# Moving elementwise work between VectorE, ScalarE and GpSimd in an attention and feed-forward kernel on 8 cores

## The chip, the cores and the metric

The kernel runs on 8 cores of one Trainium2 chip. Each core computes 1024 of the 8192 rows of the input by itself; the cores exchange nothing. The time is the device time of the slowest core in microseconds (us). Below, TensorE is PE, VectorE is DVE, ScalarE is ACT, GpSimd is POOL and SyncE is SP, as in the profile's rows.

## What is computed

```python
x = L0_attn_query_input                                   # (2, 4096, 2048) float32
x = x + attn(layernorm(x))
x = x + ffn(layernorm(x))

def attn(query_input):                                    # 16 heads of 128, 1024 stored patterns
    q = (rms_norm(query_input, nqw) @ W_in.T).reshape(B, S, H, D) @ W_q.T
    k = stored_patterns @ W_k.T
    v = stored_patterns @ W_v.T
    probs = softmax(einsum(q * sigmoid(beta), k))
    return rms_norm(einsum(probs, v), norm_retrieved_w) + query_input

def ffn(x):                                               # int8 weights with scales, 8192 wide
    return (silu(x @ w_gate * s_gate) * (x @ w_up * s_up)) @ w_down * s_down
```

## The kernel before

The program has seven stages, one after another, and between two of them stands `barrier()` (lines 201 to 217): PE, ACT and DVE each issue one tiny instruction and wait until all three have. Every engine's instructions are written out by hand in queue order (`Rt` puts one on PE's queue, `Rs` on ACT's, `Rv` on DVE's, `Rg` on POOL's, `Ry` on SP's), and every dependence is a semaphore that counts up: `cT` for PE, `cS` for ACT, `cV` for DVE, `cG` for POOL, and `vv` and `ss` for chains inside DVE and ACT. Nothing is reordered at run time: an engine that waits holds up all that stands behind it on its queue.

1. Layer norm of x, its transpose, and the product of W_in and W_q.
2. The q projection (lines 451 to 495). 16 blocks `hc`, each 32 matmuls of 128x512 into a ring of four PSUM tiles of 1024 floats; each tile is then read out by one ACT instruction (line 491) that multiplies by `bvec` (the sigmoid of beta) and writes bf16. PE waits for the readout of block hc-4 before it writes the same tile.
3. k and v of all heads.
4. Attention, head by head.
5. What is called the G stage here (lines 668 to 919): the divided softmax, the second RMS norm, the sums with x, the layer norm of the feed-forward part and its transpose, for 8 tiles `j` of 128 rows.
6. Gate and up projections, 64 blocks (lines 921 to 989).
7. Down projection in 4 quarters of 512 columns, with the last sum and the stores of the output (lines 991 to 1110).

The G stage is a software pipeline. Iteration k works on tiles k, k-1 and k-2 and puts this on the queues:

- DVE: `G_V2(k-1)` (lines 766 and 768, two instructions of one column: the mean square and its reciprocal), `G_BN(k-2)` (four bn_stats, lines 838 and 834, one bn_aggr, two instructions of one column, the last on line 845), `G_P1(k)` (lines 727 and 721: 12 of the 16 heads of the tile, 128 columns each, times the reciprocal of the softmax sum), `G_T3(k-1)` (line 788, one scalar_tensor_tensor of 2048 columns), the left half of the sum `G_AD(k-1)` (line 802, 1024 columns), `G_SE(k-2)` (line 898, the readout of the transposed tile).
- ACT: `G_sqrt(k-1)` (775), `G_SQ(k-2)` (lines 854, 858, 862 with one column and 870, the normalised tile), `G_xar(k)` (709), `G_P1s(k)` (lines 747 and 741: the other 4 heads), `G_S1(k)` (758: the sum of squares).
- POOL: the right half of the sum `G_AD(k-1)` (line 813, 1024 columns).
- PE: `G_T1(k-2)` (lines 888 and 884, 16 transposes). SP: loads of x and stores of the sum to `x1sp`.

The waits that tie them together: `G_V2(k-1)` waits for `G_S1(k-1)` on ACT; `G_BN(k-2)` waits for both halves of the sum of tile k-2; `G_SQ(k-2)` on ACT waits for `G_BN(k-2)`, and `G_xar(k)`, `G_P1s(k)` and `G_S1(k)` stand behind it on ACT's queue; `G_T3(k-1)` stands behind `G_P1(k)` on DVE's queue; the sum of tile k-1 waits for `G_T3(k-1)`.

Of the kernel before, what the change touches and what calls it, by code (L numbers as in the profile page):

```python
# [12 lines left out]
AF = mybir.ActivationFunctionType  # L13
ALU = mybir.AluOpType
# [7 lines left out]
H = 16  # L22
# [23 lines left out]
def _build_nc():  # L46
# [26 lines left out]
    with ctx:  # L73
# [12 lines left out]
        bvec = ctx.enter_context(nc.sbuf_tensor("bvec_s", [128, 1], F32))  # L86
# [88 lines left out]
        dX = [sems["dX0"], sems["dX1"]]  # L175
        dSo = [sems["dSo0"], sems["dSo1"]]
        sXr = [sems["sXr%d" % i] for i in range(4)]
        cT = sems["cT"]
        cS = sems["cS"]
        cV = sems["cV"]  # L180
        cG = sems["cG"]
# [8 lines left out]
        def Rs(f): ops["s"].append(f)  # L190

        def Rv(f): ops["v"].append(f)
# [5 lines left out]
        def wait(R, sem, val):  # L198
            R(lambda En, h=sem.h, v=val: En.wait_ge(h, v))
# [50 lines left out]
        t = cS.tick()  # L250
# [4 lines left out]
        t = cT.tick()  # L255
# [3 lines left out]
        t = cV.tick()  # L259
# [196 lines left out]
        qT = bfv(O_QT, 16384)  # L456
        q_evac_val = [None] * H
        nqw_val = [None] * EC
        for ec in range(EC):
            t = cS.tick()  # L460
# [3 lines left out]
        for hc in range(H):  # L464
            pq = PS[:, (hc % 4) * 1024:(hc % 4) * 1024 + 1024]
            if hc == 1:
                wait(Rt, cS, nqw_val[EC - 1])
            if hc >= 4:
                wait(Rt, cS, q_evac_val[hc - 4])
            for half in range(2):  # L470
                for ec in range(EC):
                    if hc == 0 and half == 0:
                        wait(Rt, cS, nqw_val[ec])
                    lastmm = half == 1 and ec == EC - 1
                    if lastmm:
                        t1 = cT.tick()
                        Rt(lambda En, pq=pq, ec=ec, half=half, hc=hc:
                           En.matmul(pq[:, half * 512:half * 512 + 512],
                                     W2T3[:, ec, hc * 128:(hc + 1) * 128],
                                     nqT3[:, ec, half * 512:half * 512 + 512],  # L480
                                     start=(ec == 0), stop=(ec == EC - 1)).then_inc(cT.h, 1))
                    else:
                        Rt(lambda En, pq=pq, ec=ec, half=half, hc=hc:
                           En.matmul(pq[:, half * 512:half * 512 + 512],  # L484
                                     W2T3[:, ec, hc * 128:(hc + 1) * 128],
                                     nqT3[:, ec, half * 512:half * 512 + 512],
                                     start=(ec == 0), stop=(ec == EC - 1)))
            wait(Rs, cT, t1)
            t2 = cS.tick()
            Rs(lambda En, hc=hc, pq=pq:  # L490
               En.activation(qT[:, hc * 1024:(hc + 1) * 1024], pq, AF.Identity,
                             scale=bvec[:]).then_inc(cS.h, 1))
            q_evac_val[hc] = t2
        barrier()

# [204 lines left out]
        def G_xar(j):  # L700
            xre = f32v(O_XRE[j % 2], 2048)
            xar = f32v(O_XA[j % 2], 2048)
            wait(Rs, sA[j % 2], g_ld[j])
            if j >= 2:
                wait(Rs, cG, adv_g[j - 2])
                wait(Rs, cV, adv_v[j - 2])
            t = cS.tick()
            Rs(lambda En, xar=xar, xre=xre, j=j:
               En.activation(xar, xre, AF.Identity, scale=a1s[:, j:j + 1],
                             bias=bbs[:, j:j + 1]).then_inc(cS.h, 1))  # L710
            xaval[j] = t

        def G_P1(j):
            t0 = f32v(O_T0[j % 2], 2048)
            if j >= 2:
                wait(Rv, cS, sq1val[j - 2])
            for hh in range(4, H):
                if hh == H - 1:
                    t = cV.tick()
                    Rv(lambda En, j=j, hh=hh, t0=t0:  # L720
                       En.tensor_scalar(t0[:, hh * 128:(hh + 1) * 128],
                                        A3[:, j, hh * 128:(hh + 1) * 128],
                                        rscol[:, hh * NT + j:hh * NT + j + 1], None,
                                        ALU.mult).then_inc(cV.h, 1))
                else:
                    Rv(lambda En, j=j, hh=hh, t0=t0:
                       En.tensor_scalar(t0[:, hh * 128:(hh + 1) * 128],
                                        A3[:, j, hh * 128:(hh + 1) * 128],
                                        rscol[:, hh * NT + j:hh * NT + j + 1], None,
                                        ALU.mult))  # L730
            p1val[j] = t

        def G_P1s(j):
            t0 = f32v(O_T0[j % 2], 2048)
            if j >= 2:
                wait(Rs, cV, t3val[j - 2])
            for hh in range(4):
                if hh == 3:
                    t = ss.tick()
                    Rs(lambda En, j=j, hh=hh, t0=t0:  # L740
                       En.activation(t0[:, hh * 128:(hh + 1) * 128],
                                     A3[:, j, hh * 128:(hh + 1) * 128], AF.Identity,
                                     scale=rscol[:, hh * NT + j:hh * NT + j + 1]).then_inc(ss.h, 1))
                    p1sval[j] = t
                else:
                    Rs(lambda En, j=j, hh=hh, t0=t0:
                       En.activation(t0[:, hh * 128:(hh + 1) * 128],
                                     A3[:, j, hh * 128:(hh + 1) * 128], AF.Identity,
                                     scale=rscol[:, hh * NT + j:hh * NT + j + 1]))
# [42 lines left out]
        def G_AD(j):  # L792
            t3r = f32v(O_T3[j % 2], 2048)
            xar = f32v(O_XA[j % 2], 2048)
            x1t = f32v(O_X1[j % 2], 2048)
            if j >= 2:
                wait(Rv, cS, x1nval[j - 2])
                wait(Rv, dX[j % 2], dxval[j - 2])
            wait(Rv, cV, t3val[j])
            t = cV.tick()  # L800
            Rv(lambda En, x1t=x1t, t3r=t3r, xar=xar:
               En.tensor_add(x1t[:, 0:1024], t3r[:, 0:1024],
                             xar[:, 0:1024]).then_inc(cV.h, 1))
            adv_v[j] = t
            wait(Rg, cV, t3val[j])
            wait(Rg, cS, xaval[j])
            if j >= 2:
                wait(Rg, cV, bnval[j - 2])
                wait(Rg, cS, x1nval[j - 2])
                wait(Rg, dX[j % 2], dxval[j - 2])  # L810
            t = cG.tick()
            Rg(lambda En, x1t=x1t, t3r=t3r, xar=xar:
               En.tensor_add(x1t[:, 1024:2048], t3r[:, 1024:2048],  # L813
                             xar[:, 1024:2048]).then_inc(cG.h, 1))
            adv_g[j] = t

        def G_SP(j):
            x1t = f32v(O_X1[j % 2], 2048)
            wait(Ry, cV, adv_v[j])
            wait(Ry, cG, adv_g[j])  # L820
            dma(Ry, dX[j % 2], x1sp_d[j], x1t)
            dxval[j] = dX[j % 2].n

        def G_BN(j):
            x1t = f32v(O_X1[j % 2], 2048)
            W = 32 + j * 16
            ST = 176 + (j % 2) * 24
            wait(Rv, cG, adv_g[j])
            wait(Rv, cV, adv_v[j])
            for i in range(4):  # L830
                if i == 3:
                    t = vv.tick()
                    Rv(lambda En, i=i, x1t=x1t, ST=ST:
                       En.bn_stats(wrk[:, ST + i * 6:ST + (i + 1) * 6],
                                   x1t[:, i * 512:(i + 1) * 512]).then_inc(vv.h, 1))
                else:
                    Rv(lambda En, i=i, x1t=x1t, ST=ST:
                       En.bn_stats(wrk[:, ST + i * 6:ST + (i + 1) * 6],
                                   x1t[:, i * 512:(i + 1) * 512]))
            wait(Rv, vv, t)  # L840
            bnval[j] = VC(
                lambda En, W=W, ST=ST: En.bn_aggr(wrk[:, W + 6:W + 8], wrk[:, ST:ST + 24]),
                lambda En, W=W: En.tensor_scalar(wrk[:, W + 8:W + 9], wrk[:, W + 7:W + 8],
                                                 EPS_LN, None, ALU.add),
                lambda En, W=W: En.reciprocal(wrk[:, W + 9:W + 10], wrk[:, W + 8:W + 9]),
                final=cV)

        def G_SQ(j):
# [15 lines left out]
            wait(Rs, ss, t)  # L864
            if j >= 2:
                wait(Rs, cT, tr2_val[j - 2])
            wait(Rs, cV, adv_v[j])
            t = cS.tick()
            Rs(lambda En, x1n=x1n, x1t=x1t, W=W:
               En.activation(x1n, x1t, AF.Identity, scale=wrk[:, W + 10:W + 11],  # L870
# [311 lines left out]
```

## Time and profile before

| | us |
|---|---|
| time of the kernel, median of 2 runs (2129.28 to 2130.96) | 2130.12 |
| time of the profiled execution | 2131.07 |
| span of its slowest core (core 5), first to last instruction | 2129.5 |
| spans of the eight cores | 2110.6 to 2129.5 |
| PE busy | 1804.7 (85%) |
| ACT busy | 633.1 (30%) |
| DVE busy | 211.1 (10%) |
| POOL busy | 176.3 (8%) |

A span runs from the first to the last instruction of one core; the time of the profiled execution is 1.6 us more than the span of its slowest core. A busy share over the whole span is a mean over seven stages with different limits: how an engine that is busy 8% of the span can still matter is read from the stage in which it works.

### The profile page before, as it was taken

Reading aid. Unit: us, or ns where it says so; the run is one execution under the profiler, and the core shown is the slowest. Engines: PE = TensorE matmul, PEld = TensorE weight load, DVE = VectorE, ACT = ScalarE, POOL = GpSimd, SP = SyncE. Lnnn points to the kernel's source line nnn. Section 1 sums busy time; section 2 is a strip of 40 time slices with the busy share of each in tenths; the row PEclk is TensorE's granted clock in tenths of the full one; section 3 lists DMA queues with packets and bytes.
Section 4 is the critical chain, followed back from the end, with each engine's and each line's share of the span. In section 5 each row is a group of like instructions: output and inputs, shape, how many; then the busy total and the mean of one; then the engine's idle time right before and its main releaser. Section 6 shows DMA issues by size and latency. Waiting matters only on the chain.

```text
span 2129.5 us, 20649 instructions; the slowest of 8 cores (2110.6 to 2129.5 us)
## 1 busy us (share of the span) xinstructions
PE 1804.7 (85%) x8489; PEld 840.0 (39%) x8489; DVE 211.1 (10%) x448; ACT 633.1 (30%) x605; POOL 176.3 (8%) x239
## 2 busy tenths in 40 slices
PE   3489778888801799999999999999997979899795
PEld 2434333443401344444444444444443434344342
DVE  3300000000068100000000000000000020100202
ACT  4741365566556111111111111111114212222120
POOL 3200110000012100000000000000000010100101
PEclk8679768888855799999999999999998989999898
DMA  9600310000053212222221222222213131221301
GB/s 284 195 1 1 98 61 0 1 1 1 1 197 119 92 66 79 80 80 79 79 72 67 79 79 80 79 79 69 70 60 104 40 104 40 79 65 40 104 20 60
DMA packets 42370, 154.67 MB, mean 73 GB/s; under 512 B 6181, under 2 KB 6182, under 8 KB 36902
## 3 DMA queue, kind: packets, MB, share of 16 engines
q0 software_dynamic: 23984, 84.00, 11.6%
q1 hardware_dynamic: 18294, 69.35, 10.2%
q8 instruction: 69, 1.13, 0.2%
q14 instruction: 23, 0.19, 0.0%
HBM read 103.10 MB, written 16.78 MB: 56 GB/s over the span
## 4 chain that ended last, share of the span: by engine, by line
PE 79%; ACT 8%; DMA 6%; DVE 4%; issue 3%; POOL 1%; SPq 0%; DVEq 0%; ACTq 0%; POOLq 0%
PE PS L955 21%; PE PS L970 20%; PE PS L1095 19%; PE PS L484 5%; PE PS L578 3%; PE PS L593 3%; DMA out<-arena 2%; DMA arena<-patT 2%; ACT arena L622 2%; PE PS L642 1%; PE PS L615 1%; PE PS L609 1%; ACT arena L332 1%; ACT arena L404 1%; ACT arena L461 1%
## 5 line engine op out<-in xcount | busy, mean ns | idle before, releaser
L1095 PE MATMUL PS<-arena 128*128 128x512 bf16 x1956 | 451.3, 386 | 48.8 <-DVE arena L1034 39.8
L955 PE MATMUL PS<-arena 128*128 128x512 bf16 x2048 | 455.2, 381 | 5.3 <-DMA arena<-wu 5.3
L970 PE MATMUL PS<-arena 128*128 128x512 bf16 x1984 | 438.7, 379 | 0.0
L1095 PEld LDWEIGHTS PS<-arena 128*128 128x128 bf16 x1956 | 193.3, 99 | 291.6 <-issue 68.4
L955 PEld LDWEIGHTS PS<-arena 128*128 128x128 bf16 x2048 | 201.0, 98 | 248.9 <-issue 9.0
L979 ACT ACTIVATE arena<-PS,sgc_s 128x1024 bf16<-128x1024 f32 x64 | 71.3, 1114 | 735.5 <-PE PS L964 735.5
L970 PEld LDWEIGHTS PS<-arena 128*128 128x128 bf16 x1984 | 194.1, 98 | 234.1
L1062 ACT ACTIVATE arena<-arena 128x2048 bf16<-128x2048 int8 x64 | 121.6, 1908 | 345.0 <-PE PS L1084 336.6
L622 ACT ACTIVATE arena<-PS 128x1024 bf16<-128x1024 f32 x128 | 129.3, 1024 | 63.1 <-PE PS L609 63.1
L987 DVE TENSOR_TENSOR arena<-arena 128x1024 bf16<-128x1024 bf16 x64 | 44.3, 693 | 851.3 <-ACT arena L982 851.3
L484 PE MATMUL PS<-arena 128*128 128x512 bf16 x496 | 117.0, 390 | 8.2 <-ACT arena L461 8.2
L578 PE MATMUL PS<-arena,onemat_s 128*128 128x512 bf16 x256 | 85.8, 420 | 18.5 <-ACT arena L622 18.5
L232 POOL DMA_DIRECT2D arena<-wg x64 | 33.9, 529 | 807.2 <-PE PS L964 795.6
L888 PE MATMUL PS<-ident_s,arena 128*128 128x128 bf16 x120 | 14.1, 309 | 102.0 <-ACT arena L870 102.0
L593 PE MATMUL PS<-arena 128*128 128x512 bf16 x240 | 82.3, 423 | 0.0
L484 PEld LDWEIGHTS PS<-arena 128*128 128x128 bf16 x496 | 49.0, 99 | 73.4 <-issue 17.9
L982 ACT ACTIVATE arena<-PS,suc_s 128x1024 bf16<-128x1024 f32 x64 | 70.9, 1107 | 0.0
L1029 DVE TENSOR_TENSOR arena<-PS,arena 128x512 f32<-128x512 f32 x32 | 22.1, 691 | 473.1 <-PE PS L1084 436.6
L615 PE MATMUL PS<-arena 128*128 128x512 bf16 x128 | 58.0, 453 | 0.1
L609 PE MATMUL PS<-arena 128*128 128x512 bf16 x128 | 57.9, 452 | 0.0
L232 POOL DMA_DIRECT2D out<-arena x32 | 17.4, 543 | 486.0 <-DVE arena L1034 484.3
L813 POOL TENSOR_TENSOR arena<-arena 128x1024 f32<-128x1024 f32 x8 | 25.6, 3194 | 384.3 <-DVE arena L788 384.3
(110 smaller groups left out, 937.3 us busy)
## 6 DMA issues: line engine op xcount, KB each, us to landing
arena<-wg POOLq DMA_DIRECT2D x64, 512.0 KB, 3.5
arena<-wu POOLq DMA_DIRECT2D x64, 512.0 KB, 4.2
arena<-win SPq DMA_DIRECT2D x16, 1024.0 KB, 7.4
arena<-x SPq DMA_DIRECT2D x16, 1024.0 KB, 8.5
arena<-wd SPq DMA_DIRECT2D x64, 256.0 KB, 2.7
arena<-patT SPq DMA_DIRECT2D x16, 512.0 KB, 4.4
x1sp<-arena SPq DMA_DIRECT2D x8, 1024.0 KB, 4.2
arena<-x1sp POOLq DMA_DIRECT2D x32, 256.0 KB, 5.0
```

Of the source, the lines that this page charges most:

```text
L484: En.matmul(pq[:, half * 512:half * 512 + 512], W2T3[:, ec, hc * 128:(hc + 1) * 128], nqT3[:, ec, half * 512:half * 512 + 512], start=(ec ...
L578: En.matmul(PSS[:, half * 512:half * 512 + 512], onemat[:], eT[:, m * 1024 + half * 512:m * 1024 + half * 512 + 512], start=(m == 0), stop ...
L593: En.matmul(PU[:, half * 512:half * 512 + 512], vsb[:, (h * MC + m) * 128:(h * MC + m + 1) * 128], eT[:, m * 1024 + half * 512:m * 1024 + ...
L609: En.matmul(psb[:, half * 512:half * 512 + 512], kT[:, h * 1024 + mc * 128:h * 1024 + (mc + 1) * 128], qT[:, h * 1024 + half * 512:h * 102 ...
L615: En.matmul(psb[:, half * 512:half * 512 + 512], kT[:, h * 1024 + mc * 128:h * 1024 + (mc + 1) * 128], qT[:, h * 1024 + half * 512:h * 102 ...
L622: En.activation(eT[:, mc * 1024:(mc + 1) * 1024], psb, AF.Exp).then_inc(cS.h, 1))
L955: En.matmul(PG[:, half * 512:half * 512 + 512], wgb[:, hc * 128:(hc + 1) * 128], x1nT3[:, hc, half * 512:half * 512 + 512], start=(hc == 0 ...
L970: En.matmul(PU2[:, half * 512:half * 512 + 512], wub[:, hc * 128:(hc + 1) * 128], x1nT3[:, hc, half * 512:half * 512 + 512], start=(hc == ...
L979: En.activation(sgb, PG, AF.Silu, scale=sgc[:, ic:ic + 1]))
L982: En.activation(sub, PU2, AF.Identity, scale=suc[:, ic:ic + 1]).then_inc(cS.h, 1))
L1062: En.activation(wdb, wd8, AF.Copy).then_inc(cS.h, 1))
L1095: En.matmul(PS[:, j * 512:(j + 1) * 512], fuse3[:, ic, j * 128:(j + 1) * 128], wdb[:, c * 512:(c + 1) * 512], start=(ic == 0), stop=(ic == ...
```

## The change

It edits stages 2 and 5.

In stage 2 the 16 readouts of the q tiles go from ACT to DVE: line 491 becomes a `tensor_scalar` of 1024 columns from PSUM, and PE waits for `cV` in place of `cS`.

In the G stage `G_P1` keeps 9 heads on DVE instead of 12, and `G_P1s` does 7 on ACT instead of 4. DVE's half of the sum (line 802) is gone, and POOL adds all 2048 columns in one instruction (line 803 of the changed kernel). The waits for DVE's half are dropped or turned to POOL's counter: `adv_v[j]` now holds the value of `cG`.

```diff
             if hc >= 4:
-                wait(Rt, cS, q_evac_val[hc - 4])
+                wait(Rt, cV, q_evac_val[hc - 4])
...
-            wait(Rs, cT, t1)
-            t2 = cS.tick()
-            Rs(lambda En, hc=hc, pq=pq:
-               En.activation(qT[:, hc * 1024:(hc + 1) * 1024], pq, AF.Identity,
-                             scale=bvec[:]).then_inc(cS.h, 1))
+            wait(Rv, cT, t1)
+            t2 = cV.tick()
+            Rv(lambda En, hc=hc, pq=pq:
+               En.tensor_scalar(qT[:, hc * 1024:(hc + 1) * 1024], pq, bvec[:], None,
+                                ALU.mult).then_inc(cV.h, 1))
...
                 wait(Rs, cG, adv_g[j - 2])
-                wait(Rs, cV, adv_v[j - 2])
...
-            for hh in range(4, H):
+            for hh in range(7, H):
...
-            for hh in range(4):
-                if hh == 3:
+            for hh in range(7):
+                if hh == 6:
...
-            if j >= 2:
-                wait(Rv, cS, x1nval[j - 2])
-                wait(Rv, dX[j % 2], dxval[j - 2])
-            wait(Rv, cV, t3val[j])
-            t = cV.tick()
-            Rv(lambda En, x1t=x1t, t3r=t3r, xar=xar:
-               En.tensor_add(x1t[:, 0:1024], t3r[:, 0:1024],
-                             xar[:, 0:1024]).then_inc(cV.h, 1))
-            adv_v[j] = t
...
-               En.tensor_add(x1t[:, 1024:2048], t3r[:, 1024:2048],
-                             xar[:, 1024:2048]).then_inc(cG.h, 1))
+               En.tensor_add(x1t, t3r, xar).then_inc(cG.h, 1))
             adv_g[j] = t
+            adv_v[j] = t
...
-            wait(Ry, cV, adv_v[j])
             wait(Ry, cG, adv_g[j])
...
             wait(Rv, cG, adv_g[j])
-            wait(Rv, cV, adv_v[j])
...
-            wait(Rs, cV, adv_v[j])
+            wait(Rs, cG, adv_g[j])
```

DVE's queue in one steady iteration of the G stage, before, from `G_P1` to the next `G_BN` (each row is an instruction, what it writes and reads, and the semaphores it waits for):

```order
L727 TENSOR_SCALAR arena<-arena,rscol_s 128x128 [waits cS]
L727 TENSOR_SCALAR arena<-arena,rscol_s 128x128 x10
L721 TENSOR_SCALAR arena<-arena,rscol_s 128x128
L788 SCALAR_TENSOR_TENSOR arena<-arena,wrk_s 128x2048 [waits ss,dC,cG]
L802 TENSOR_TENSOR arena<-arena 128x1024 [waits cS,dX0,cV]
L898 COPY arena<-PS 128x16x128 [waits cT]
L766 TENSOR_SCALAR wrk_s<-wrk_s 128x1 [waits cS]
```

The same place in the changed kernel, where the line numbers have shifted (727 is 726, 721 is 720, 788 is 787, 898 is 886, 766 is 765, 768 is 767, 838 is 826):

```order
L726 TENSOR_SCALAR arena<-arena,rscol_s 128x128 [waits cS]
L726 TENSOR_SCALAR arena<-arena,rscol_s 128x128 x7
L720 TENSOR_SCALAR arena<-arena,rscol_s 128x128
L787 SCALAR_TENSOR_TENSOR arena<-arena,wrk_s 128x2048 [waits ss,dC]
L886 COPY arena<-PS 128x16x128 [waits cT]
L765 TENSOR_SCALAR wrk_s<-wrk_s 128x1 [waits cS]
L767 RECIPROCAL wrk_s<-wrk_s 128x1 [waits vv]
L826 BN_STATS wrk_s<-arena 128x6 [waits cG]
```

Three of the 128-column products and the sum of 1024 columns have left the queue, and bn_stats waits for POOL's counter alone.

ACT's queue in one steady iteration, before, from the normalised tile of `G_SQ` to the square root:

```order
L870 ACTIVATE arena<-arena,wrk_s 128x2048 [waits ss,cT,cV]
L709 ACTIVATE arena<-arena,bbs_s,a1s_s 128x2048 [waits sA0,cG,cV]
L747 ACTIVATE arena<-arena,rscol_s 128x128 [waits cV]
L747 ACTIVATE arena<-arena,rscol_s 128x128 x2
L741 ACTIVATE arena<-arena,rscol_s 128x128
L758 ACTIVATE arena,wrk_s<-arena 128x2048 [waits cV,ss]
L775 ACTIVATE wrk_s<-wrk_s 128x1 [waits cV]
```

And in the changed kernel (870 is 858, 709 is 708, 747 is 746, 741 is 740, 758 is 757, 775 is 774):

```order
L858 ACTIVATE arena<-arena,wrk_s 128x2048 [waits ss,cT,cG]
L708 ACTIVATE arena<-arena,bbs_s,a1s_s 128x2048 [waits sA0,cG]
L746 ACTIVATE arena<-arena,rscol_s 128x128 [waits cV]
L746 ACTIVATE arena<-arena,rscol_s 128x128 x5
L740 ACTIVATE arena<-arena,rscol_s 128x128
L757 ACTIVATE arena,wrk_s<-arena 128x2048 [waits cV,ss]
L774 ACTIVATE wrk_s<-wrk_s 128x1 [waits cV]
```

Three products more stand between the normalised tile and the sum of squares; the order is otherwise as it was.

## Rows read from the trace of the kernel before

**Rows 1.** The page: the chain that ended last, by engine.
```profile
PE 79%; ACT 8%; DMA 6%; DVE 4%; issue 3%; POOL 1%; SPq 0%; DVEq 0%; ACTq 0%; POOLq 0%
```

**Rows 2.** Windows, core 5: stretch, length, busy us (instructions) by engine, PEclk, DMA, GB/s.
```profile
587.25:705.50 118.25, 14.92 (x128) 13.02 (x128) 83.26 (x193) 66.71 (x98) 25.55 (x8) 0.50 0.41 151
...
635.55:647.97 12.42, 1.86 (x16) 1.63 (x16) 10.38 (x24) 8.15 (x12) 3.16 (x1) 0.50 0.45 165
```

**Rows 3.** Waits in the G stage: who waited for whom, us in total, times, longest.
```profile
ACT wrk_s L854 <- DVE wrk_s L845: 30.3, 8, 6.8
DVE wrk_s L766 <- ACT arena L758: 22.1, 8, 12.0
...
DVE wrk_s L838 <- POOL arena L813: 1.0, 1, 1.0
```

**Rows 4.** Timeline of DVE, one steady iteration: start, us, what [idle before <-releaser].
```profile
635.55 1.88 DVE L838 BATCH_NORM_STATS2 wrk_s<-arena 128x6 f32<-128x512 f32 x3
...
638.86 2.25 DVE L727 TENSOR_SCALAR arena<-arena,rscol_s 128x128 f32<-128x128 bf16 x11
641.02 0.28 DVE L721 TENSOR_SCALAR arena<-arena,rscol_s 128x128 f32<-128x128 bf16 x1
641.22 2.35 DVE L788 SCALAR_TENSOR_TENSOR arena<-arena,wrk_s 128x2048 f32<-128x2048 f32 x1
643.67 1.23 DVE L802 TENSOR_TENSOR arena<-arena 128x1024 f32<-128x1024 f32 x1
644.81 1.22 DVE L898 COPY arena<-PS 128x2048 bf16<-128x2048 bf16 x1
647.55 0.15 DVE L766 TENSOR_SCALAR wrk_s<-wrk_s 128x1 f32<-128x1 f32 x1 [1.52 <-ACT arena L758]
```

**Rows 5.** Timeline of ACT, the same iteration.
```profile
639.01 0.20 ACT L854 ACTIVATE wrk_s<-wrk_s 128x1 f32<-128x1 f32 x1 [3.17 <-DVE wrk_s L845]
...
640.10 2.09 ACT L870 ACTIVATE arena<-arena,wrk_s 128x2048 bf16<-128x2048 f32 x1 [0.20 <-ACT wrk_s L862]
...
644.08 0.97 ACT L747 ACTIVATE arena<-arena,rscol_s 128x128 f32<-128x128 bf16 x3
644.96 0.39 ACT L741 ACTIVATE arena<-arena,rscol_s 128x128 f32<-128x128 bf16 x1
645.44 1.91 ACT L758 ACTIVATE arena<-arena 128x2048 f32<-128x2048 f32 x1
```

**Rows 6.** Timeline of POOL: the first sum, one of a steady iteration, the last.
```profile
606.97 3.32 POOL L813 TENSOR_TENSOR arena<-arena 128x1024 f32<-128x1024 f32 x1 [322.18 <-DVE arena L788]
...
643.95 3.16 POOL L813 TENSOR_TENSOR arena<-arena 128x1024 f32<-128x1024 f32 x1 [9.21 <-DVE arena L788]
...
691.48 3.14 POOL L813 TENSOR_TENSOR arena<-arena 128x1024 f32<-128x1024 f32 x1 [7.05 <-DVE arena L788]
```

**Rows 7.** Timeline of DVE at the first and at the last tiles.
```profile
606.86 1.23 DVE L802 TENSOR_TENSOR arena<-arena 128x1024 f32<-128x1024 f32 x1
...
610.46 1.88 DVE L838 BATCH_NORM_STATS2 wrk_s<-arena 128x6 f32<-128x512 f32 x3 [0.95 <-POOL arena L813]
...
685.30 1.88 DVE L838 BATCH_NORM_STATS2 wrk_s<-arena 128x6 f32<-128x512 f32 x3
...
691.20 1.23 DVE L802 TENSOR_TENSOR arena<-arena 128x1024 f32<-128x1024 f32 x1
...
695.31 1.87 DVE L838 BATCH_NORM_STATS2 wrk_s<-arena 128x6 f32<-128x512 f32 x3
```

**Rows 8.** Groups by line and shape, POOL, core 5: busy us, mean ns | idle before.
```profile
L303 POOL CAST arena<-arena 128x2048 bf16<-128x2048 f32 x16 | 30.3, 1893 | 57.7 <-DMA arena<-win 37.1 <-PE PS L318 20.6
...
L517 POOL CAST arena<-arena 128x1024 bf16<-128x1024 f32 x16 | 16.6, 1040 | 176.8 <-DMA arena<-patT 176.8
```

**Rows 9.** Groups by line and shape: ACT and DVE of core 5, then DVE of core 0.
```profile
L491 ACT ACTIVATE arena<-PS,bvec_s 128x1024 bf16<-128x1024 f32 x16 | 17.8, 1114 | 92.7 <-PE PS L478 92.7
...
L1029 DVE TENSOR_TENSOR arena<-PS,arena 128x512 f32<-128x512 f32 x32 | 22.1, 691 | 473.1 <-PE PS L1084 436.6 <-DMA out<-arena 36.4
...
L1029 DVE TENSOR_TENSOR arena<-PS,arena 128x512 f32<-128x512 f32 x32 | 22.1, 690 | 480.6 <-PE PS L1084 432.6 <-DMA out<-arena 48.0
```

## The prediction

> **What bounds the kernel now.** I read the chain that ended last first: PE holds 79% of it, ACT 8%, DVE 4%, POOL 1% [rows 1]. The matmul stages are PE's, and the change takes nothing from PE. What it moves lies in two places, so I read these: the end of stage 2, and the G stage, from 587.25 to 705.5 us. There PE is busy 14.92 of 118.25 us, DVE 83.26, ACT 66.71, POOL 25.55 [rows 2]. No engine is near full: the stage is set by a loop of waits. The waits name it: ACT waits 8 times, 30.3 us in all, for DVE's line 845 (end of `G_BN`), DVE waits 8 times, 22.1 us, for ACT's line 758 (`G_S1`), and only once, 1.0 us, for POOL [rows 3].
>
> One steady iteration takes 12.42 us [rows 2]. I count from the start of bn_stats at 635.55 [rows 4]. ACT's line 854 starts 3.46 us later, at 639.01, the normalised tile at 640.10, the product of heads at 644.08, the sum of squares at 645.44 [rows 5]; DVE's line 766, released by it, at 647.55 [rows 4]; the next bn_stats starts 0.42 us behind it, at 647.97, the end of the window in [rows 2]. So the loop is `G_BN` on DVE, then `G_SQ`, `G_xar`, `G_P1s`, `G_S1` on ACT, then `G_V2` on DVE. The other DVE work of the iteration (`G_P1`, `G_T3`, its half of the sum, `G_SE`) stands beside it: DVE is through with it at 646.03 and idles 1.52 us [rows 4].
>
> **The change part by part.**
>
> *Three heads from DVE to ACT.* On ACT the products start 0.293 us apart (644.08 to 644.96 for three [rows 5]), so three more make 0.88 us, inside the loop. On DVE they start 0.196 us apart (638.86 to 641.02 for eleven [rows 4]); taking three away makes 0.59 us, but outside it. The loop through ACT goes from 12.42 to 13.30 us. Nothing covers the 0.88: ACT idles 3.17 us per iteration [rows 5], but ahead of line 854, and the products stand behind it on the same queue.
>
> *DVE's half of the sum.* Line 802 took 1.23 us [rows 4] beside the loop, followed by an idle DVE. Taking it away gives nothing directly.
>
> *The whole sum on POOL.* This adds a path: `G_BN` must wait for a POOL instruction twice as wide. How long is that? The trace shows only the half: 3.32, 3.16 and 3.14 us [rows 6]. But each ran beside line 802. The first, 606.97 to 610.29, began 0.11 us after line 802, which ended at 608.09; the others, at 643.95 and 691.48, began 0.28 us after it [rows 4, 6, 7]. From the end of line 802 to the end of POOL's half it is 2.20, 2.21 and 2.19 us. A longer overlap makes the instruction longer by exactly as much, so POOL did no work while line 802 ran. I read 2.20 us as the work on 1024 columns, and 4.40 us as that on 2048, since in the changed kernel no line 802 exists.
>
> The Trainium skill ("SBUF — State Buffer", section "Who interferes with whom") has a rule for this: a DVE instruction with two SBUF inputs and a GpSimd instruction that reads SBUF exclude each other for the whole instruction. By that rule the 2.20 us stand; the trace agrees. Its "GPSIMD Engine Reference" (section 3.1) gives 4.50 us for an fp32 add of 2048 columns; with that as an estimate the sum below would be 0.2 us more.
>
> Bounds: if part of the 2.20 is paid once, as in the casts (1.893 us for 2048 columns, 1.040 for 1024 [rows 8], so 0.19 us is fixed), the sum takes 4.21 us. If there is no exclusion and POOL is just slow, it is twice 3.15, 6.30 us. I take 4.40: it is twice what three rows agree on. Shorter than 4.21 is excluded, since it has twice the columns to do.
>
> Path through POOL, from bn_stats: `G_T3` starts after 5.67 us (641.22 minus 635.55), now 0.59 earlier, 5.08; POOL starts 2.73 us after that (643.95 minus 641.22); it runs 4.40; bn_stats follows 0.17 us after its end (610.29 to 610.46 [rows 6, 7]). Sum 12.38 us. That is 0.92 less than the 13.30 through ACT: in the steady iterations POOL is hidden, and it would decide from a duration of 5.32 us on.
>
> *Fill and drain,* where POOL is not hidden:
> - First bn_stats (610.46 before, released by POOL [rows 7]). ACT's products of tile 0 push all by 0.88, DVE's fewer products pull `G_T3(0)` by 0.59, so POOL starts at 606.97 + 0.29 = 607.26, ends at 611.66, and bn_stats starts at 611.83: +1.37 us.
> - Six iterations up to the seventh bn_stats at 685.30: 6 x 0.88 = +5.28 us.
> - Last bn_stats: 10.01 us after the seventh (695.31 [rows 7]). POOL starts as before at 691.48, 6.18 us after the seventh, then 4.40 and 0.17: 10.75. +0.74 us.
>
> Together +7.39 us. SP's load of tile k+2 stands ahead of the store that waits for POOL, and the store behind it is released by the same event as bn_stats, so SP delays nobody.
>
> *The q readout on DVE.* PE fills a tile in some 6.9 us and has a ring of four, so 15 of 16 readouts are covered; the last stands before a barrier. ACT takes 1.114 us [rows 9]. DVE with a PSUM input takes 0.691 us for 512 columns [rows 9], and line 802 1.23 for 1024 without PSUM [rows 7]: I take 1.23, +0.11 us. Bounds: 0.69 (if it runs at twice the rate) to 1.38 (twice 0.691): -0.42 to +0.27. No DVE work is queued there, so its wait holds up nobody.
>
> Sum: +7.5 us on the profiled 2131.07, 2138.6. That execution lies 0.95 us above the median of the runs, so the forecast is 2137.6.
>
> **The rivals.**
>
> A. *POOL is the new bound.* Without exclusion the sum takes 6.30 us; the iteration becomes 7.98 + 6.30 = 14.28, +1.86 six times, 11.2; the first bn_stats comes 1.37 + 1.90 = 3.3 later, the last 0.74 + 1.90 = 2.6 more. +17.1 us, with the readout 2147.3. For it: the half really took 3.15. Against it: the three rows that end 2.20 us after line 802. It decides above 5.32 us.
>
> B. *DVE is the bound of the G stage,* and not slower comes out: it is the busiest engine there with 83.26 us [rows 2], and 0.59 + 1.23 us leave it per tile. Eight tiles would give 14.6 us back: 2115.5. It decides if DVE, once released, has no idle time. Against it: the 1.52 us idle in each iteration and the 22.1 us of waits for ACT [rows 3, 4]. Removing work from an engine that waits gives nothing.
>
> C. *The waits for output stores in the last stage shift.* DVE waited 36.4 us there on core 5 and 48.0 us on core 0 of the same run [rows 9], and both ended within 0.5 us of each other. All cores reach this stage some 7 us later, so a shift in common should leave these waits alone; if they don't, up to 11.6 us go either way: 2126 to 2149. It cancels the loss only from 7.5 us on.
>
> **How the numbers follow.** Forecast (2135 to 2140.5, the bounds of POOL's 4.21 and the readout, and 2 us for run and store waits): 0.70. Rival A 0.15. Rival B 0.04. Rival C 0.10, half to each side. Something not named here 0.01. The range 2132 to 2148.5 takes in A and parts of C. The kernel's measurement tells about 2% from no change, 42.6 us: faster would be below 2087.5, slower above 2172.7, and no case reaches either. So faster 0.01, within 0.98, slower 0.01.
>
> **What would show it.** Right: in the G stage ACT's line 757 is followed by an iteration of 13.3 us; seven products 0.293 us apart; POOL's line 803 takes 4.4 us and DVE waits for it only at the first and last tile; the stage is 7 to 8 us longer; the last q readout takes 1.2 us. Wrong: bn_stats waits for POOL in every iteration (rival A), a period at or below 12.4 us (rival B), or a G stage that is 7 us longer with a total that isn't (rival C). The forecast falls if POOL's sum takes over 5.3 us, or if the ACT products of an iteration fit into its idle time.

## The result and the profile after

The changed kernel is slower by a third of a per cent, far less than the 2% from which the measurement tells a change. The median of its 11 runs is 2139.07 us, that of 10 runs of the kernel before, made beside them, 2133.54 us. Some executions of either kernel are 1.5 to 13% longer, with a lower granted clock; they are in these medians, and the ratio is taken without them: 1.0036, 95% interval 1.0025 to 1.0047, which is +7.7 us (5.3 to 10.0). The forecast was +7.5 us, 2137.6.

The profiled execution took 2132.41 us, less than any of the 11 runs and only 1.3 us more than the profile before, so its total says little. Measured from one barrier matmul of PE (line 208) to the next and averaged over the cores, the G stage grew from 117.6 to 125.2 us, the last stage shrank from 528.6 to 525.0, and every other stretch agrees within 0.4 us. In the nine profiles of the experiments the last stage took 526.2 to 529.1 us, so the small total is that stage's scatter. Of the G stage's 7.7 us, 1.0 lies in the wait for the first load of x, which scatters too (7.7 to 11.3 us from the barrier, by core). Behind this load the stage's length agrees within 0.1 us on all eight cores of an execution. I therefore read the change from there. The stage is measured from the start of ACT's first `xar` (line 709, in the changed kernel 708), which waits for the load of x, to PE's closing barrier matmul (line 208). Timeline of the kernel before, core 5:

```profile
596.27 2.09 ACT L709 ACTIVATE arena<-arena,bbs_s,a1s_s 128x2048 f32<-128x2048 f32 x1 [9.43 <-DMA arena<-x]
...
705.53 0.16 PE L208 MATMUL PS<-onesrow_s 1*1 1x1 bf16 x1 [1.48 <-DVE arena L898]
```

and of the changed kernel, core 2, the slowest of its profile:

```profile
595.58 2.09 ACT L708 ACTIVATE arena<-arena,bbs_s,a1s_s 128x2048 f32<-128x2048 f32 x1 [10.81 <-DMA arena<-x]
...
711.53 0.16 PE L208 MATMUL PS<-onesrow_s 1*1 1x1 bf16 x1 [1.48 <-DVE arena L886]
```

That is 109.26 us before and 115.95 after: +6.69 us. The chain of the whole program is PE's as before [rows 1]:

```profile
PE 78%; ACT 8%; DMA 5%; DVE 4%; issue 3%; POOL 1%; SPq 0%; DVEq 0%; ACTq 0%; POOLq 0%
```

Windows over the stage and over one iteration (columns as in [rows 2]: length, then busy us of PE, PE's weight loads, DVE, ACT, POOL):

```profile
585.00:711.60 126.60, 15.08 (x130) 13.09 (x129) 69.09 (x161) 73.71 (x122) 36.07 (x8) 0.50 0.37 141
624.43:637.60 13.17, 1.87 (x16) 1.63 (x16) 8.59 (x22) 9.03 (x15) 4.51 (x1) 0.50 0.41 151
```

DVE's work per iteration fell from 10.38 to 8.59 us and ACT's rose from 8.15 to 9.03 [rows 2], and the iteration grew from 12.42 to 13.17. The busiest engine was relieved and the stage got longer. The waits say why; against [rows 3]:

```profile
DVE wrk_s L765 <- ACT arena L757: 35.4, 8, 14.9
ACT wrk_s L842 <- DVE wrk_s L833: 30.1, 8, 7.6
...
DVE wrk_s L826 <- POOL arena L803: 1.4, 2, 0.7
```

DVE waits 13.3 us more for ACT than before, ACT as long as before for DVE, and for POOL DVE waits twice, 1.4 us in all, not in every iteration. One iteration on DVE, against [rows 4]:

```profile
624.43 1.88 DVE L826 BATCH_NORM_STATS2 wrk_s<-arena 128x6 f32<-128x512 f32 x3
...
627.74 1.66 DVE L726 TENSOR_SCALAR arena<-arena,rscol_s 128x128 f32<-128x128 bf16 x8
...
629.50 2.35 DVE L787 SCALAR_TENSOR_TENSOR arena<-arena,wrk_s 128x2048 f32<-128x2048 f32 x1
633.13 1.22 DVE L886 COPY arena<-PS 128x2048 bf16<-128x2048 bf16 x1 [1.28 <-PE PS L872]
637.24 0.15 DVE L765 TENSOR_SCALAR wrk_s<-wrk_s 128x1 f32<-128x1 f32 x1 [2.89 <-ACT arena L757]
```

and on ACT, against [rows 5]:

```profile
627.89 0.20 ACT L842 ACTIVATE wrk_s<-wrk_s 128x1 f32<-128x1 f32 x1 [3.10 <-DVE wrk_s L833]
...
632.91 1.84 ACT L746 ACTIVATE arena<-arena,rscol_s 128x128 f32<-128x128 bf16 x6
634.66 0.38 ACT L740 ACTIVATE arena<-arena,rscol_s 128x128 f32<-128x128 bf16 x1
635.13 1.91 ACT L757 ACTIVATE arena<-arena 128x2048 f32<-128x2048 f32 x1
```

ACT's wait of 3.1 us stands where it stood, ahead of line 842 (854 before), and all seven products lie behind it: from the first product to the sum of squares it is 2.22 us, before 1.36. POOL's sums, first, steady and last, against [rows 6]:

```profile
606.65 4.50 POOL L803 TENSOR_TENSOR arena<-arena 128x2048 f32<-128x2048 f32 x1 [322.70 <-DVE arena L787]
...
632.24 4.51 POOL L803 TENSOR_TENSOR arena<-arena 128x2048 f32<-128x2048 f32 x1 [8.84 <-DVE arena L787]
...
696.69 4.50 POOL L803 TENSOR_TENSOR arena<-arena 128x2048 f32<-128x2048 f32 x1 [7.09 <-DVE arena L787]
```

and bn_stats on DVE at the first, the seventh and the last tile, against [rows 7]:

```profile
611.25 1.88 DVE L826 BATCH_NORM_STATS2 wrk_s<-arena 128x6 f32<-128x512 f32 x3 [0.70 <-POOL arena L803]
...
690.51 1.88 DVE L826 BATCH_NORM_STATS2 wrk_s<-arena 128x6 f32<-128x512 f32 x3
...
701.29 1.88 DVE L826 BATCH_NORM_STATS2 wrk_s<-arena 128x6 f32<-128x512 f32 x3 [0.69 <-POOL arena L803]
```

Twice the columns took 4.50 us, not twice 3.15. The end of stage 2:

```profile
235.80 0.38 PE L478 MATMUL PS<-arena 128*128 128x512 bf16 x1
236.29 1.28 DVE L491 TENSOR_SCALAR arena<-PS,bvec_s 128x1024 bf16<-128x1024 f32 x1 [5.62 <-PE PS L478]
...
237.72 0.16 PE L208 MATMUL PS<-onesrow_s 1*1 1x1 bf16 x1 [1.54 <-DVE arena L491]
```

PE stood 1.54 us for the last readout; on the kernel before it was 1.47 us for ACT's.

### The profile page after: what moved, and what is told of

The parts are those of the page before. It is cut to its first block, busy times and chain, and to the rows that moved or that the text cites. A ratio compares the mean times of both kernels' runs of the same rounds, so it can differ in the third digit from the quotient of the medians.

```text
span 2130.9 us, 20446 instructions; the slowest of 8 cores (2121.1 to 2130.9 us)
## 1 busy us (share of the span) xinstructions
PE 1790.3 (84%) x8336; PEld 840.4 (39%) x8489; DVE 217.7 (10%) x432; ACT 622.6 (29%) x613; POOL 186.8 (9%) x239
## 3 DMA queue, kind: packets, MB, share of 16 engines
q8 instruction: 69, 1.13, 0.2%
## 4 chain that ended last, share of the span: by engine, by line
PE 78%; ACT 8%; DMA 5%; DVE 4%; issue 3%; POOL 1%; SPq 0%; DVEq 0%; ACTq 0%; POOLq 0%
PE PS L943 21%; PE PS L958 20%; PE PS L1083 19%; PE PS L484 5%; PE PS L578 3%; PE PS L593 2%; DMA out<-arena 2%; DMA arena<-patT 2%; ACT arena L622 2%; PE PS L642 1%; PE PS L609 1%; PE PS L615 1%; ACT arena L332 1%; ACT arena L404 1%; ACT arena L461 1%
## 5 line engine op out<-in xcount | busy, mean ns | idle before, releaser
L1083 PE MATMUL PS<-arena 128*128 128x512 bf16 x1919 | 446.8, 384 | 50.7 <-DVE arena L1022 39.2
L943 PE MATMUL PS<-arena 128*128 128x512 bf16 x2007 | 451.6, 380 | 7.9 <-DMA arena<-wu 5.8
L958 PE MATMUL PS<-arena 128*128 128x512 bf16 x1943 | 435.7, 379 | 2.1
L622 ACT ACTIVATE arena<-PS 128x1024 bf16<-128x1024 f32 x128 | 129.2, 1024 | 61.5 <-PE PS L609 61.5
L484 PE MATMUL PS<-arena 128*128 128x512 bf16 x485 | 115.7, 389 | 9.2 <-ACT arena L461 8.8
L593 PE MATMUL PS<-arena 128*128 128x512 bf16 x239 | 81.3, 419 | 0.1
L803 POOL TENSOR_TENSOR arena<-arena 128x2048 f32<-128x2048 f32 x8 | 36.1, 4509 | 381.2 <-DVE arena L787 381.2
L609 PE MATMUL PS<-arena 128*128 128x512 bf16 x128 | 57.5, 449 | 1.9 <-issue 1.5
L876 PEld LDWEIGHTS PS<-ident_s,arena 128*128 128x128 bf16 x120 | 12.2, 143 | 111.8 <-issue 111.8
```

Source lines behind the costliest of these rows:

```text
L484: En.matmul(pq[:, half * 512:half * 512 + 512], W2T3[:, ec, hc * 128:(hc + 1) * 128], nqT3[:, ec, half * 512:half * 512 + 512], start=(ec ...
L593: En.matmul(PU[:, half * 512:half * 512 + 512], vsb[:, (h * MC + m) * 128:(h * MC + m + 1) * 128], eT[:, m * 1024 + half * 512:m * 1024 + ...
L609: En.matmul(psb[:, half * 512:half * 512 + 512], kT[:, h * 1024 + mc * 128:h * 1024 + (mc + 1) * 128], qT[:, h * 1024 + half * 512:h * 102 ...
L622: En.activation(eT[:, mc * 1024:(mc + 1) * 1024], psb, AF.Exp).then_inc(cS.h, 1))
L943: En.matmul(PG[:, half * 512:half * 512 + 512], wgb[:, hc * 128:(hc + 1) * 128], x1nT3[:, hc, half * 512:half * 512 + 512], start=(hc == 0 ...
L958: En.matmul(PU2[:, half * 512:half * 512 + 512], wub[:, hc * 128:(hc + 1) * 128], x1nT3[:, hc, half * 512:half * 512 + 512], start=(hc == ...
```

## The experiments

The theory under test is that of the prediction: the stage's period (the time from one tile's first bn_stats to the next tile's) is that of the longest of several loops of waits, here the one through ACT; the path through POOL is the next, 0.9 us shorter; and POOL does no work while DVE runs an instruction with two SBUF inputs. In the tables "first" is from the stage's start to the first tile's bn_stats, "six" the six periods from there to the seventh, "last" from the seventh to the eighth; the figures are the same on all cores within 0.1 us. The last two kernels and the one with the q readout alone were run once each, so they have no ratio.

| kernel | first | six | last | stage |
|---|---|---|---|---|
| before | 14.19 | 74.84 | 10.01 | 109.26 |
| changed | 15.67 | 79.26 | 10.78 | 115.95 |
| heads alone | 14.99 | 80.01 | 10.00 | 115.22 |
| sum alone | 15.30 | 78.21 | 10.77 | 114.53 |
| q readout alone | 14.18 | 74.76 | 10.01 | 109.18 |
| changed, with a two-input add on DVE | 16.66 | 79.55 | 11.58 | 118.03 |
| changed, with one-input work on DVE | 15.68 | 79.45 | 10.79 | 116.15 |

**The heads alone.**

```diff
-            for hh in range(4, H):
+            for hh in range(7, H):
...
-            for hh in range(4):
-                if hh == 3:
+            for hh in range(7):
+                if hh == 6:
```

Expected, as written before the run:

> Kernel before with the heads alone moved (9 on DVE, 7 on ACT); the sum stays split, the q readout stays on ACT. All stage figures below: from the start of ACT's first line 709 in the G stage to PE's closing barrier matmul; before 109.3 us, changed kernel 115.9. Theory (the loop through ACT sets the period, three products of 0.293 us are inside it): period 12.47 -> 13.2-13.3 us, stage +5.2 us. Rival (DVE bounds the stage, so relieving it by 0.59 us per tile helps): period about 11.9 us, stage -4 us. Rival (ACT's 3.1 us of idle time take the three products in): no change.

Measured: ratio 1.0034 (1.0018 to 1.0051); periods of 13.24 to 13.30 us and one of 13.64, stage +5.96 us (expected +5.2, which left out the first tile's +0.80). DVE has 0.59 us less to do per tile and the stage is longer: the rival that DVE bounds it (B) is out, and so is the one in which ACT's idle time takes the products in. The six periods are 5.17 us longer, 0.86 each; the usual one goes from 12.42 to 13.30 us, +0.88, which is the three products of 0.293 us.

**The sum alone.** The kernel before with `G_AD`, `G_SP`, `G_BN`, `G_xar` and `G_SQ` as in the changed kernel, and heads 12 and 4:

```diff
-               En.tensor_add(x1t[:, 1024:2048], t3r[:, 1024:2048],
-                             xar[:, 1024:2048]).then_inc(cG.h, 1))
+               En.tensor_add(x1t, t3r, xar).then_inc(cG.h, 1))
```

> Kernel before with the sum alone moved: POOL adds all 2048 columns, DVE's half is gone, heads 12 and 4, q readout on ACT. Theory (two paths compete, the longer sets the period; POOL's sum takes 4.5 us and, with 12 heads on DVE ahead of it, the path through POOL is 5.67+2.73+4.51+0.17 = 13.1 us, over ACT's 12.4): bn_stats waits for POOL in every iteration, period 13.1 us, first bn_stats +1.2, last +0.8, stage +5.6 us. So the two edits cost 5.2 and 5.6 us apart and 6.7 together: they don't add up. Rival (POOL is hidden in steady iterations under either split, costs at both ends only): period 12.4, stage +2 us.

Measured: ratio 1.0033 (1.0018 to 1.0049); stage +5.27 us. In this kernel DVE does wait for POOL in the steady iterations; DVE and then POOL in the timeline:

```profile
637.39 1.88 DVE L826 BATCH_NORM_STATS2 wrk_s<-arena 128x6 f32<-128x512 f32 x3 [1.00 <-POOL arena L803]
...
643.05 2.35 DVE L787 SCALAR_TENSOR_TENSOR arena<-arena,wrk_s 128x2048 f32<-128x2048 f32 x1
...
650.40 1.88 DVE L826 BATCH_NORM_STATS2 wrk_s<-arena 128x6 f32<-128x512 f32 x3 [0.59 <-POOL arena L803]
```

```profile
645.79 4.51 POOL L803 TENSOR_TENSOR arena<-arena 128x2048 f32<-128x2048 f32 x1 [8.50 <-DVE arena L787]
```

As expected (13.1), the period is 13.01 us (637.39 to 650.40), of which 5.66 lie ahead of line 787, 2.74 to POOL's start, 4.51 in POOL and 0.10 behind it. With 12 heads ahead of `G_T3` the path through POOL is the longest; with 9 it is 0.59 us shorter and ACT's has grown past it. Alone the two edits cost 5.96 and 5.27 us, together 6.69: each lengthens another path, and only the longer of two counts. The rival of this run, that POOL is hidden under any split, is out.

**The q readout alone.**

```diff
-            wait(Rs, cT, t1)
-            t2 = cS.tick()
+            wait(Rv, cT, t1)
+            t2 = cV.tick()
```

with `tensor_scalar` in place of the activation, and PE's wait on `cV`.

> Kernel before with the q readout alone on DVE. Theory: 15 of 16 readouts lie beside matmuls; from the end of the last matmul of stage 2 to the barrier matmul 1.54 instead of 1.47 us, nothing else moves; DVE's instruction takes 1.28 us. Rival (the readout on DVE holds PE up at the ring of four): gaps between the blocks of 32 matmuls, over 0.1 us each.

Measured in one execution, 2134.53 us: PE waits 1.54 us for the last readout, which takes 1.28 us, and blocks of 32 matmuls follow each other without a gap at the block's start. The G stage is 0.08 us shorter. The readout costs 0.07 us (1.54 instead of 1.47), too little to be seen in a total; the rival, gaps between the blocks, is out.

**A two-input add on DVE beside POOL's whole sum.** The changed kernel, and in `G_AD`:

```diff
+            scr = f32v(O_SQG[1], 1024)
+            wait(Rv, cS, xaval[j])
+            wait(Rv, cV, t3val[j])
+            t = cV.tick()
+            Rv(lambda En, scr=scr, t3r=t3r, xar=xar:
+               En.tensor_add(scr, t3r[:, 0:1024], xar[:, 0:1024]).then_inc(cV.h, 1))
```

and `G_xar(j)` waits for the add of tile j-2. The result of the add is not used.

> Changed kernel with a DVE tensor_add of 1024 columns more per tile, two SBUF inputs, into unused SBUF, at the place where DVE's half of the sum stood. Theory (a DVE instruction with two SBUF inputs and POOL's sum exclude each other): POOL's sum gets longer by the overlap, 4.51 + 0.95 to 1.12 = 5.45 to 5.6 us, and its end lies 4.35 to 4.5 us after the end of DVE's instruction; the path through POOL passes ACT's (threshold 5.3 us), bn_stats waits for POOL in every iteration, period 13.3 to 13.5 us. Rival (POOL's rate is what it is, and the 2.20 us was chance): POOL's sum stays at 4.5 us and the period at 13.2.

Measured, DVE and POOL of a steady iteration:

```profile
642.74 1.23 DVE L814 TENSOR_TENSOR arena<-arena 128x1024 f32<-128x1024 f32 x1
...
648.08 0.15 DVE L768 TENSOR_SCALAR wrk_s<-wrk_s 128x1 f32<-128x1 f32 x1 [2.78 <-ACT arena L760]
...
648.44 1.88 DVE L836 BATCH_NORM_STATS2 wrk_s<-arena 128x6 f32<-128x512 f32 x3
```

```profile
603.18 5.48 POOL L806 TENSOR_TENSOR arena<-arena 128x2048 f32<-128x2048 f32 x1 [320.37 <-DVE arena L790]
...
643.02 5.31 POOL L806 TENSOR_TENSOR arena<-arena 128x2048 f32<-128x2048 f32 x1 [7.91 <-DVE arena L790]
```

POOL's same 2048 columns take 5.31 us instead of 4.51, and end 4.36 us after the end of DVE's add (643.97), so the exclusion is there. The stretch is 0.80 us where the overlap is 0.95: some 0.15 us of POOL's instruction run beside DVE, which I had not counted. So 5.31 falls just short of the 5.32 from which POOL decides: its end at 648.33 lies 0.11 us ahead of bn_stats at 648.44, and where bn_stats does wait for POOL it starts 0.10 us behind it. The expectation missed here: the period stays at 13.22 us instead of the 13.3 to 13.5 expected (with one of 13.42, which the next run has too), and the first and the last tile pay most of it: +0.99 and +0.80 us of the stage's +2.08.

**The same place, one-input work on DVE.** In place of the add stand two bn_stats, and `G_xar(j)` waits for them as it did for the add.

```diff
+            for i in range(2):
...
+                       En.bn_stats(scr6[:, i * 6:i * 6 + 6],
+                                   t3r[:, i * 512:(i + 1) * 512])
```

> Changed kernel with two bn_stats of 512 columns more per tile on DVE (one SBUF input each, about 1.2 us together), into unused SBUF, at the place of the tensor_add of the run with two inputs. Theory (only a second SBUF input excludes POOL): POOL's sum stays at 4.51 us, period 13.2 us, stage as in the changed kernel. Rival (any DVE work beside POOL slows it): POOL's sum gets longer by about a microsecond and the period passes 13.3 us.

Measured:

```profile
641.43 0.69 DVE L818 BATCH_NORM_STATS2 arena<-arena 128x6 f32<-128x512 f32 x1
642.04 0.68 DVE L814 BATCH_NORM_STATS2 arena<-arena 128x6 f32<-128x512 f32 x1
```

```profile
641.72 4.52 POOL L806 TENSOR_TENSOR arena<-arena 128x2048 f32<-128x2048 f32 x1 [8.65 <-DVE arena L790]
```

POOL keeps its 4.5 us, and the stage is 0.20 us longer, by one period of 13.42. The pair of runs shows that it is not DVE's being busy that stops POOL. The add differs from bn_stats in its second SBUF input and in the 1024 columns that it writes; DVE's readout writes 2048 columns to SBUF beside every sum of POOL but the first in the changed kernel (line 886 at 646.47, POOL from 645.41 for 4.51 us) and doesn't slow it. The second input is what is left. It isn't the whole condition, as the products below show.

**Another order of the queues.** If the stage is bound by a loop of waits and by no engine, an order that takes work out of the loop must shorten it. In a first version ACT does `G_xar(k)`, `G_P1s(k)` and `G_S1(k)` ahead of `G_SQ(k-2)`, and DVE does `G_SE(k-3)`, `G_T3(k-1)`, `G_BN(k-2)`, `G_P1(k+1)`. The instructions are the same.

```diff
+        G_P1(0)
         for k in range(NT + 2):
             if 0 <= k - 1 < NT:
                 G_V2(k - 1)
                 G_sqrt(k - 1)
-            if 0 <= k - 2 < NT:
-                G_BN(k - 2)
-                G_SQ(k - 2)
-                G_T1(k - 2)
             if k < NT:
                 G_xar(k)
-                G_P1(k)
                 G_P1s(k)
                 G_S1(k)
+            if k <= NT and 0 <= k - 3 < NT:
+                G_SE(k - 3)
...
                 G_T3(k - 1)
                 G_AD(k - 1)
...
+            if 0 <= k - 2 < NT:
+                G_BN(k - 2)
+                G_SQ(k - 2)
+                G_T1(k - 2)
+            if k + 1 < NT:
+                G_P1(k + 1)
```

On the changed kernel (with `G_P1(j)` waiting also for `G_T3(j-2)`):

> Changed kernel with the G stage's queues in another order: on ACT xar, the seven products and the sum of squares of tile k stand ahead of the normalised tile k-2; on DVE the readout (tile k-3), T3(k-1), bn_stats (k-2), and the products of tile k+1 one iteration early. Same instructions. Theory (the stage is a loop of waits, no engine is full; once ACT's work of tile k no longer waits for bn_stats of tile k-2, the period falls to DVE's own work of about 9.1 us plus gaps): period 9.3 to 10 us, stage 90 us against 109.3 before, whole kernel 19 us under before, ratio 0.991. Rival (ACT or POOL is full once the loop is gone): period stays above 12 us, ratio about 1.0.

On the kernel before:

> The same order of the queues on the kernel before (12 and 4 heads, the sum split). Theory: DVE's own work is now the bound, 10.4 us busy per tile plus gaps: period about 11.0 us, stage about 98 us, ratio 0.995. So the work moved by the change is worth 1.3 to 1.5 us per tile here, where it cost 0.8 in the old order. Rival (where the work sits doesn't matter even then): both orders give the same period.

| kernel | first | six | last | stage | ratio to before (95%) |
|---|---|---|---|---|---|
| first order, changed | 20.14 | 73.70 | 5.07 | 109.15 | 0.9991 (0.9969 to 1.0014) |
| first order, before | 20.16 | 81.21 | 3.37 | 114.98 | 1.0013 (0.9991 to 1.0035) |

Both missed: periods of 12.3 and 13.4 to 13.6 us instead of 9.3 to 10 and 11. Timeline of DVE and POOL, first order on the changed kernel:

```profile
650.62 3.06 DVE L727 TENSOR_SCALAR arena<-arena,rscol_s 128x128 f32<-128x128 bf16 x8
...
656.39 1.22 DVE L887 COPY arena<-PS 128x2048 bf16<-128x2048 bf16 x1 [2.19 <-PE PS L873]
657.53 2.34 DVE L788 SCALAR_TENSOR_TENSOR arena<-arena,wrk_s 128x2048 f32<-128x2048 f32 x1
```

```profile
647.72 4.50 POOL L804 TENSOR_TENSOR arena<-arena 128x2048 f32<-128x2048 f32 x1 [7.75 <-DVE arena L788]
```

I had built a new loop: the readout of tile k-3 stood ahead of `G_T3` on DVE's queue, and waited for PE, PE for ACT's normalised tile, that for bn_stats of the iteration before. On the kernel before the same loop holds DVE's half of the sum too, 1.14 us more (line 802 at 651.81, bn_stats at 652.95). And the products, 1.66 us in the changed kernel, took 3.06 here, which cost nothing, since DVE idles 2.19 us behind them. The view of that line alone shows one of them (durations min/median/max):

```profile
L727 DVE TENSOR_SCALAR arena<-arena,rscol_s x8: 273/274/1687, 650.6 to 653.4; 128x128 f32<-128x128 bf16 x8
```

It is the first of them, and ran from 650.62 to 652.31, 0.09 us beyond the end of POOL's sum at 652.22. DVE's `tensor_scalar` of 128 columns is shut out by POOL too, though it has one SBUF input.

**A second order.** The readout goes behind bn_stats and ahead of the products, so that bn_stats and readout, which POOL doesn't hold up, lie beside POOL's sum:

```diff
-            if k <= NT and 0 <= k - 3 < NT:
-                G_SE(k - 3)
...
                 G_BN(k - 2)
                 G_SQ(k - 2)
                 G_T1(k - 2)
+            if 0 <= k - 3 < NT:
+                G_SE(k - 3)
             if k + 1 < NT:
                 G_P1(k + 1)
```

> Changed kernel with a second order of the G stage's queues: as in the first reordered run, but DVE's readout of the transposed tile k-3 stands behind bn_stats (k-2) instead of ahead of T3(k-1), and the nine products of tile k+1 stand last. In the first reordered run T3 waited for the readout, that for PE, PE for ACT, ACT for bn_stats (a new loop, 12.3 us), and DVE's first product ran 1.69 us instead of 0.27, up to the end of POOL's sum. Theory (both are mended: the readout's tile was finished an iteration earlier, and bn_stats and readout, 4.5 us, cover POOL's sum of 4.5 us): the loop left is bn_stats, SQ, square root, T3: 3.4 + 3.6 + 0.3 + 2.6 = about 9.9 us; stage about 93 us against 109.26 before, whole kernel 16 us under before, ratio 0.992; no product over 0.3 us. Rival (the stage has no slack to give, some engine is full near 12 us): period over 12 us, ratio 1.0.

> The same second order on the kernel before (12 and 4 heads, sum split between DVE and POOL). Theory (DVE is full now): 1.15 us of its half of the sum and 0.59 us of three products more on DVE: period about 11.0 to 11.6 us, stage about 100 us, ratio 0.995 to 0.996. The move of work that cost 0.8 us per tile in the old order is worth over 1 us per tile in this one. Rival (the split doesn't matter in this order either): period equal to that of the changed kernel's split within 0.2 us.

| kernel | first | six | last | stage | ratio to before (95%) |
|---|---|---|---|---|---|
| second order, changed | 20.14 | 58.00 | 5.07 | 93.45 | 0.9931 (0.9918 to 0.9944) |
| second order, before | 20.15 | 66.75 | 4.43 | 101.56 | 0.9962 (0.9948 to 0.9976) |

Timeline of DVE, second order on the changed kernel:

```profile
639.58 2.35 DVE L788 SCALAR_TENSOR_TENSOR arena<-arena,wrk_s 128x2048 f32<-128x2048 f32 x1 [0.54 <-ACT wrk_s L775]
641.85 1.87 DVE L827 BATCH_NORM_STATS2 wrk_s<-arena 128x6 f32<-128x512 f32 x3
...
645.14 1.22 DVE L887 COPY arena<-PS 128x2048 bf16<-128x2048 bf16 x1
646.29 2.01 DVE L727 TENSOR_SCALAR arena<-arena,rscol_s 128x128 f32<-128x128 bf16 x8
...
649.36 2.35 DVE L788 SCALAR_TENSOR_TENSOR arena<-arena,wrk_s 128x2048 f32<-128x2048 f32 x1 [0.54 <-ACT wrk_s L775]
```

```profile
642.32 4.52 POOL L804 TENSOR_TENSOR arena<-arena 128x2048 f32<-128x2048 f32 x1 [5.26 <-DVE arena L788]
```

The period is 9.78 us, as expected within 0.2, and the rival (an engine full near 12 us) is out. DVE idles 0.54 us of it, ahead of `G_T3`; DVE is busy 8.82 us and ACT 8.97, so both are now near full. The expected path through `G_SQ` and DVE's own queue are about equally long: on core 3 the square root at 650.08 follows `G_SQ`, those at 640.31 and 659.85 wait 0.3 us for DVE. One expectation missed, that no product takes over 0.3 us: the products still take 2.01 us instead of 1.66, since POOL ends at 646.84 and they start at 646.29. In the same order on the kernel before, DVE idles as little but has its half of the sum and three products more:

```profile
634.21 1.22 DVE L803 TENSOR_TENSOR arena<-arena 128x1024 f32<-128x1024 f32 x1
635.35 1.87 DVE L839 BATCH_NORM_STATS2 wrk_s<-arena 128x6 f32<-128x512 f32 x3
...
643.08 2.35 DVE L789 SCALAR_TENSOR_TENSOR arena<-arena,wrk_s 128x2048 f32<-128x2048 f32 x1 [0.54 <-ACT wrk_s L776]
...
646.68 1.87 DVE L839 BATCH_NORM_STATS2 wrk_s<-arena 128x6 f32<-128x512 f32 x3
```

11.33 us. So the same move of work costs 0.75 us per tile in the old order (12.42 to 13.17) and gains 1.55 in the new one (11.33 to 9.78). The second order on the changed kernel beats the kernel before by 0.69% (14.7 us of 2129.66, with a stage 15.8 us shorter), and so the changed kernel too, which was 0.36% slower than the kernel before, though it and the changed kernel were not run side by side.

## Why the prediction was right

- *The bound.* The loop through ACT, and not DVE's work. Right: relieving DVE by 1.8 us per tile lengthened the stage, and the heads alone did it too.
- *Three products on ACT, 0.88 us in the loop.* Right: with the heads alone the usual period is the forecast 13.30 us. In the changed kernel it is 13.23, and the six together grew by 4.42 us, not 5.28, the largest error in the sum. Two parts of it can be read. bn_stats follows line 765 after 0.36 us instead of 0.42 (ACT's wait of 3.10 instead of 3.17 is the same 0.06), which makes 0.4 us in six; bn_stats has a wait less in the changed kernel, and with the heads alone, where it keeps both, it is 0.42. And one period of the kernel before is 12.73 us, where DVE stands idle for 0.47 us between bn_stats and bn_aggr (line 842); the changed kernel shows no such pause, some of the others have one at another tile (a period of 13.64 with the heads alone), and what makes it is open.
- *POOL's whole sum, 4.40 us.* The step that mattered most, since from 5.32 us on POOL would have set the period. It measured 4.51, and the reason given for it, exclusion by DVE's line 802, is shown by the run in which such an add brings it back. The 4.40 is 0.1 short: "POOL did no work while line 802 ran" was not quite so, since some 0.15 us of POOL's instruction run beside it, and twice 2.20 leaves them out. The Trainium skill's rule ("SBUF — State Buffer", section "Who interferes with whom") and its 4.50 us ("GPSIMD Engine Reference", section 3.1) both agree with these traces, but for that 0.15 us.
- *Fill and drain.* +1.37 forecast, +1.48 measured; +0.74 forecast, +0.77 measured. The first is 0.1 off by POOL's 4.50.
- *The q readout.* +0.11 forecast, +0.07 measured; DVE took 1.28 us, not 1.23.
- *Sum.* 7.39 + 0.11 = 7.5 us forecast; 6.69 + 0.07 = 6.8 in the traces, +7.7 (5.3 to 10.0) in the runs. That the total came within 0.2 us of the forecast is luck: the stage came 0.7 us short of its sum, and the runs can't tell that.
- *Rivals.* A did not come (bn_stats waited for POOL twice, not each time), though the sum alone, with the heads left, does make POOL the bound, with a sum of 4.51 us and not of 6.30. B is out. C: in the pair of profiles DVE's wait for output stores did fall, on core 0 from 48.0 to 37.4 us, on core 5 from 36.4 to 36.2 [rows 9], in the mean of the cores from 38.8 to 35.8; with the last stage 3.5 us shorter this hid nearly half of the loss in that one execution. But the four profiles of the experiments that contain the whole change have a last stage of 527.2 to 529.1 us, so nothing ties it to the change; it is scatter, of the size that C named.

My first reordering missed by the same rule: I summed each engine's work and did not follow the new order round for its loops.

## What to carry to other kernels

In a stage where no engine is full, write down the loops of waits with their lengths before moving work: an instruction counts by the loop it lies in, not by how busy its engine is, and edits that lengthen different loops don't add up. An engine's idle time covers new work only if the work stands ahead of that wait on its queue; so reorder the queues first, and then balance the engines, since here the same split lost 0.75 us per tile in one order and won 1.55 in the other. And when a POOL instruction looks slow, see whether a DVE instruction with two SBUF inputs ran at its start, and measure from the end of that one.

## What the runs showed of the hardware that was not expected

- POOL's add of 2048 float32 columns takes 4.51 us with no such DVE add beside it, and 5.31 beside a DVE add with two SBUF inputs that overlaps it by 0.95 us, 5.48 with an overlap of 1.13: all but some 0.15 us of the overlap is lost. Beside bn_stats (one SBUF input) and the readout from PSUM it isn't slowed (4.52 us).
- It goes the other way too: a DVE `tensor_scalar` from bf16 in SBUF to float32 in SBUF, 128 columns, 0.27 us alone, took 1.69 us, until about the end of POOL's add. Which property of the instruction decides this was not tested. The same operation on one column was not held up: in the kernel before, line 766 ran at 609.08, 0.10 us after ACT's end, while POOL's first sum ran (606.97 to 610.29 [rows 6]).
- DVE's `tensor_scalar` of 1024 float32 columns from PSUM to bf16 takes 1.28 us, longer than ACT's 1.11 us for the same readout [rows 9].
